# First slots and drain of a cross attention: other loads, lent buffers, unread products, new order

## The reference

```python
x = x + xattn(layernorm(x), ctx, lens, Wq, Wk, Wv, Wo, q_norm_w, k_norm_w)
x = x + attn(layernorm(x), w_qkv, b_qkv, w_out, b_out)
x = x + ffn(layernorm(x), w_gate, w_up, w_down)

def xattn(q, kv, lens, ...):        # q (4, 128, 512), kv (4, 2048, 512), 16 heads of 64
    qh, kh, vh = heads(q @ Wq), heads(kv @ Wk), heads(kv @ Wv)
    qh, kh = rms_norm(qh, q_norm_w), rms_norm(kh, k_norm_w)
    scores = einsum('bhld,bhsd->bhls', qh, kh) / sqrt(64)
    scores = where(arange(2048) < lens[:, None], scores, -1e9)
    return merge(softmax(scores) @ vh) @ Wo
```

## Time and profile before

| | |
|---|---|
| median of 3 runs | 1163.91 us (1163.73 to 1163.95) |
| the profiled execution | 1166.78 us, its span 1165.0 us |
| TensorE busy | 1135.1 us, 97% |
| VectorE busy | 837.2 us, 72% |
| POOL busy | 857.9 us, 74% |
| ScalarE busy | 739.9 us, 64% |

### The profile page before, as it was taken

The page is one execution under the profiler, slowest core; times in us unless marked ns, Lnnn a source line. Parts: engine busy times, 40 slices in busy tenths (PEclk is TensorE's granted clock), DMA queues, the critical chain, the costliest instruction groups (busy, mean ns, idle before and its releaser), DMA issues. The chain is left out here.

```text
span 1165.0 us, 29367 instructions
## 1 busy us (share of the span) xinstructions
PE 1135.1 (97%) x10783; PEld 868.0 (75%) x10783; DVE 837.2 (72%) x1953; ACT 739.9 (64%) x1335; POOL 857.9 (74%) x744
## 2 busy tenths in 40 slices
PE   7999999999999999999999999999999899999988
PEld 5777778887888888788888887888887578654433
DVE  7788788797767678777677787767665654753686
ACT  6366656776776767666666777666666535823761
POOL 4599999888989888798889878988888633540600
PEclk9999999999999999999999999999999999999999
DMA  8679999999999999999999999999999924786000
GB/s 232 154 143 190 216 189 185 200 230 232 200 202 207 199 197 222 216 197 201 205 206 195 193 229 200 186 199 210 205 187 197 263 69 118 137 232 140 1 1 36
DMA packets 560573, 210.36 MB, mean 181 GB/s; under 512 B 506800, under 2 KB 525232, under 8 KB 560432
## 3 DMA queue, kind: packets, MB, share of 16 engines
q1 hardware_dynamic: 538544, 168.64, 77.8%
q10 hardware_dynamic: 21888, 39.86, 12.7%
HBM read 66.79 MB, written 23.07 MB: 77 GB/s over the span
## 5 line engine op out<-in xcount | busy, mean ns | idle before, releaser
L155 PE MATMUL pair<-arena 128*128 128x256 f16 x2048 | 560.6, 274 | 9.4 <-DVE arena L703 8.7
L156 PE MATMUL pair<-arena 128*128 128x256 f16 x2048 | 559.5, 273 | 0.0
L157 PE MATMUL pair<-arena 128*128 128x256 f16 x2048 | 559.5, 273 | 0.0
L545 POOL TENSOR_TENSOR p_parts<-probs,p_parts 128x512 f16<-128x512 f32 x256 | 314.4, 1233 | 22.7 <-ACT p_parts L652 22.0
L749 DVE CUSTOM_DVE_ANT_0 probs<-bank,mask 128x512 f32<-128x512 f32 x256 | 175.3, 685 | 157.9 <-PE bank L917 145.2
L555 POOL TENSOR_TENSOR k_rinv<-k_ms,half_neg 128x8 f32<-128x8 f32 x128 | 211.8, 1655 | 80.7 <-DVE k_ms L764 80.3
L155 PEld LDWEIGHTS pair<-arena 128*128 128x128 f16 x2048 | 200.2, 98 | 83.7 <-issue 49.2
L157 PEld LDWEIGHTS pair<-arena 128*128 128x128 f16 x2048 | 200.7, 98 | 23.8
L156 PEld LDWEIGHTS pair<-arena 128*128 128x128 f16 x2048 | 200.6, 98 | 21.1
L656 ACT ACTIVATE k_lh<-k_n 128x512 f16<-128x512 f32 x128 | 80.5, 629 | 187.9 <-DVE k_n L772 186.2
L629 ACT ACTIVATE probs<-probs,neg_max 128x512 f32<-128x512 f32 x256 | 182.9, 714 | 10.7 <-DVE neg_max L758 10.7
(11 more groups left out here) (314 smaller groups left out, 1714.6 us busy)
## 6 DMA issues: line engine op xcount, KB each, us to landing
raws<-in_ctx_t_dram SPq DMA_DIRECT2D x58, 256.0 KB, 3.7
side_kept<-side_parts ACTq DMA_DIRECT2D x40, 256.0 KB, 5.3
arena<-side_kept SPq DMA_DIRECT2D x40, 256.0 KB, 4.6
w_kept<-ffn_turned ACTq DMA_DIRECT2D x36, 256.0 KB, 3.8
side_raw<-in_w_qkv_dram ACTq DMA_DIRECT2D x24, 256.0 KB, 3.4
arena<-w_kept SPq DMA_DIRECT2D x24, 256.0 KB, 5.0
pt<-p_parts SPq DMA_TRANSPOSE x240, 4.2
ffn_raw<-in_w_gate_dram ACTq DMA_DIRECT2D x12, 256.0 KB, 3.2
```

What stands on the lines that cost most here:

```text
L155: nc.tensor.matmul(to, x_hi[k], w_hi[k], start=(k == 0), stop=False)
L156: nc.tensor.matmul(to, x_hi[k], w_lo[k], start=False, stop=False)
L157: mm = nc.tensor.matmul(to, x_lo[k], w_hi[k], start=False, stop=(k == n - 1))
L545: nc.gpsimd.tensor_tensor(p_parts[n % PTS][:, 1, :], probs[n % PROBS][:, :], p_parts[n % PTS][:, 0, :], ALU.subtract).then_inc(p_lo_done, 1)
```

## The change

- The first 22 tiles fit without waiting: 8 halves of the buffers `p_parts` and `pt` are lent besides the 10 of `probs` and 4 of `raws`. 16 are loaded at once, six more behind the transposes of x; x of batch 0 is loaded behind the sixth tile instead of the third.
- In the list the query weights move behind the tenth context tile (slots 2 and 3), and the second group's weights one slot ahead. The first query unit is projected in slot 4 instead of 2, with its square and sum in the same slot; pairs 0 and 1 are scored in slots 9 and 10 instead of 8 and 9.
- Steps of x are put on other places between the tiles, and the steps of keys 0 to 2 on VectorE and ScalarE too. Sum and scale of each query unit stand ahead of the tiles of their slot.
- TensorE runs 36 products of a zeroed buffer nobody reads, then waits for the third high part and runs 4 more.
- Drain: in slots from 257 TensorE does out projection, turns, values, then scores (before: scores, turns, values, out projection); pairs 125, 126, 127 are scored in slots 257, 258, 260. POOL splits keys 127 ahead of a part. Residual of a batch comes a slot before its statistics; batches 0 and 1 one slot earlier; transposes by one slot closer. The weights of self attention are loaded three per slot from slot 258. A loop of warming products whose range of slots (257 to before 257) is empty is removed.

```diff
 CTX_RAWS, KTS, VS, PROBS, PTS, QS = 4, 3, 10, 10, 4, 3
...
 MASKS_AT = SCORE_LAG
+FIRST_SCORES = (SCORE_LAG + 2, SCORE_LAG + 3)
+WARM_FIRST, WARM_SECOND, EARLY_KEYS = 36, 4, 3
 FREE_AT = 120
-X0_AT = (2, 4, 5)
-Q_AT = {2: (0, 0), 18: (1, 0), 22: (2, 0), 26: (3, 0), 31: (0, 1), 35: (1, 1), 39: (2, 1), 43: (3, 1)}
+X0_AT = ((-1, 5), (0, 0), (1, 0))
+Q_AT = {4: (0, 0), 18: (1, 0), 22: (2, 0), 26: (3, 0), 31: (0, 1), 35: (1, 1), 39: (2, 1), 43: (3, 1)}
 Q_UNITS = list(Q_AT.values())
-OUT_FIRST, NORM_AT, WO_FIRST = (257, 261, 265), (261, 265), 249
+OUT_FIRST, NORM_AT, WO_FIRST = (257, 261, 265), (260, 264), 249
...
+        warm = mask[:, CHUNKS - 1, 0:P].bitcast(F16)
...
             ITEMS[t // 2 - 2] = [("c", 0, t), ("c", 0, t + 1)]
+        ITEMS[2] += [("q", 0, 0), ("q", 0, 1)]
+        ITEMS[3] = [("q", 0, 2), ("q", 0, 3)] + ITEMS[3]
         for j in range(4):
-            ITEMS[j // 2].insert(j % 2, ("q", 0, j))
             ITEMS[27 + j] = [("q", 1, j)]
-        ITEMS[6] = [("w", 0, 1), ("w", 1, 1)]
+        ITEMS[5] += [("w", 0, 1), ("w", 1, 1)]
         for group in range(2, GROUPS):
...
-            return probs[j][:, :].rearrange("p (k s) -> p k s", k=KD) if j < PROBS else ctx_raw[(j - PROBS) % CTX_RAWS]
+            if j >= FIRST:
+                return ctx_raw[(j - FIRST) % CTX_RAWS]
+            if j < PROBS:
+                return probs[j][:, :].rearrange("p (k s) -> p k s", k=KD)
+            i, of_pt = divmod(j - PROBS, 2)
+            lent = pt[i][:, :, :].rearrange("p a q -> p (a q)") if of_pt else p_parts[i][:, :, :].rearrange("p a k -> p (a k)")
+            return lent.bitcast(F32).rearrange("p (k s) -> p k s", k=KD)
 
...
-            return Q_UNITS.index(Q_AT[slot - lag]) if slot - lag in Q_AT else None
+            first = min(Q_AT)
+            if slot == first + (0, 0, 0, 1, 2, 3, 4, 5)[lag]:
...
         def pair_of_scores(slot):
 
-            if slot == SCORE_LAG + 1:
-                return 0
+            if slot in FIRST_SCORES:
+                return FIRST_SCORES.index(slot)
+            if slot > PARTS:
+                return LAST_SCORES.get(slot)
             d, odd = divmod(slot - SCORE_LAG, 2)
-            return d if 0 < d < PROJS and not odd else None
...
 
-            if slot == SCORE_LAG + 2:
-                return [0, 1]
+            if slot - 1 in FIRST_SCORES:
+                d = FIRST_SCORES.index(slot - 1)
+                return [2 * d, 2 * d + 1]
+            if slot - 1 in LAST_SCORES:
+                return [2 * LAST_SCORES[slot - 1], 2 * LAST_SCORES[slot - 1] + 1]
             n = slot - SCORE_LAG - 1
-            return [n] if 2 <= n < PARTS else []
+            return [n] if 2 * len(FIRST_SCORES) <= n < 2 * min(LAST_SCORES.values()) else []
 
...
             def load(j):
-                if j >= PROBS + CTX_RAWS:
...
 
-            for j in range(PROBS + CTX_RAWS):
+            for j in range(AT_ONCE):
...
+                    if n == 0:
+                        sp.wait_ge(item_lo_done, FIRST)
...
                 for item in split(slot):
-                    if PROBS + CTX_RAWS <= no[item] + CTX_RAWS < len(item_list):
+                    if FIRST + CTX_RAWS <= no[item] + CTX_RAWS < len(item_list):
...
                         sp.dma_start_transpose(xt0[i][:, :, b * P:(b + 1) * P], x_parts[:, i, :]).then_inc(xt0_in[b], 16)
+                    if b == 0:
+                        for j in range(AT_ONCE, FIRST + CTX_RAWS):
...
-                if (b := batch_at(5, slot)) is not None:
+                if (b := batch_at(4, slot)) is not None:
...
-                for j in range(GROUPS + 2 * (slot - PARTS), GROUPS + 2 * (slot - PARTS) + 2):
+                for j in range(GROUPS + 3 * (slot - PARTS - 2), GROUPS + 3 * (slot - PARTS - 1)):
...
+            nc.gpsimd.memset(warm, 0.0).then_inc(warm_ready, 1)
...
+                d = slot // 2 - 1
+                if slot > PARTS and slot % 2 == 0 and d - 1 < PROJS:
+                    keys_low(d - 1)
...
+                if slot <= PARTS and slot % 2 == 0 and 0 <= d - 1:
+                    keys_low(d - 1)
...
-                for i, item in enumerate(split(slot)):
-                    item_high(item)
-                    if slot == -1 and i == X0_AT[2]:
-                        x_high(0)
...
                 if (m := q_unit(1, slot)) is not None:
                     act.wait_ge(qp_done, m + 1)
...
+                if slot % 2 == 1 and 0 <= d < EARLY_KEYS:
+                    keys_high(d)
+                for i, item in enumerate(split(slot)):
+                    item_high(item)
+                    if (slot, i) == X0_AT[2]:
+                        x_high(0)
...
+                    if n == 0:
+                        act.wait_ge(item_lo_done, FIRST)
...
+                if slot % 2 == 1 and EARLY_KEYS <= d < PROJS:
+                    keys_high(d)
...
+                    wait(dve, q_ms_done, m - 1)
+                    nc.vector.tensor_reduce(q_ss[m % 2][:, :], q_sq, AX_X, ALU.add).then_inc(q_ss_done, 1)
...
                 for i, item in enumerate(split(slot)):
+                    if slot % 2 == 0 and 0 <= d < EARLY_KEYS - 1 and i == len(split(slot)) // 2:
+                        keys_normed(d)
                     item_low(item)
-                    if slot == -1 and i == X0_AT[0]:
+                    if (slot, i) == X0_AT[0]:
                         x_moments(0)
-                    if slot == -1 and i == X0_AT[1]:
...
                     dve.wait_ge(norm_in, 32)
                     nc.vector.scalar_tensor_tensor(norm_w[:, :], qk_norm[:, 0, :], Q_UP, qk_norm[:, 1, :], ALU.mult,
                                                    ALU.mult).then_inc(norm_done, 1)
...
                                                    ALU.mult, ALU.add).then_inc(r_done, 1)
...
+            def out_projected(slot):
+                for b in range(len(OUT_FIRST)):
+                    first = (slot - OUT_FIRST[b]) * 2
+                    if not 0 <= first < GROUPS:
+                        continue
...
+                    if first % 4 == 0:
+                        pe.wait_ge(side_in[first // 4], 64)
+                    for k in range(first, first + 2):
+                        hi, lo = (ot[:, b, i, k, :] for i in range(2))
...
+            def unread(times):
+                for i in range(times):
+                    nc.tensor.matmul(pair[0][:, 0, :], warm[:, 0:P], warm, start=True, stop=True)
+
+            pe.wait_ge(warm_ready, 1)
+            unread(WARM_FIRST)
+            pe.wait_ge(item_hi_done, 3)
+            unread(WARM_SECOND)
             for slot in range(LAST):
...
-                if PARTS + 1 <= slot < OUT_FIRST[0]:
-                    pe.wait_ge(k_n_done, PROJS - 1)
-                    pe.wait_ge(v_lo_done, PROJS - 1)
-                    for i in range(WARM_DRAIN):
-                        nc.tensor.matmul(bank[0][:, 0:4 * VW], ident16[:, :], v_both[0][:, 0, :, :, :].rearrange("p h a v -> p (h a v)"),
-                                         start=True, stop=True)
+                if slot <= PARTS:
+                    scored(slot)
+                out_projected(slot)
...
                 if slot > PARTS:
                     values(slot)
...
+                    scored(slot)
```

More of the change, by code:

```diff
@@ L877, in values, with scored @@
                     mm.then_inc(pv_done, 1)
+            def scored(slot):
+                if (m := pair_of_scores(slot)) is not None:
+                    u = m // CHUNKS
+                    pe.wait_ge(kt_in[m % 2], 16 * (m // 2 + 1))
+                    if u == 0:
+                        pe.wait_ge(q_turned_in, 16)
+                    elif m % CHUNKS == 0:
+                        pe.wait_ge(q_in[u % QS], 16 * ((u - (u % QS == 0)) // QS + 1))
+                    wait(pe, s_max_done, 2 * m)
+                    for i, (q_part, k_part) in enumerate(((0, 0), (1, 0), (0, 1))):
+                        for h in range(2):
+                            rows = slice(HD * h, HD * (h + 1))
+                            q_now = q_turned[rows, q_part, 0, :] if u == 0 else q_st[u % QS][rows, q_part, :]
+                            mm = nc.tensor.matmul(scores[h][:, :], q_now,
+                                                  kt[m % KTS][rows, TILES * k_part:TILES * (k_part + 1), :].rearrange(
+                                                      "p t k -> p (t k)"), start=(i == 0), stop=(i == 2))
+                    mm.then_inc(s_done, 1)
```

118 lines of the change are left out of this document (52 added, 66 removed).

## The result

The changed kernel takes 1169.17 us (median of 18 runs, 1164.06 to 1174.52), the kernel before, measured beside it, 1163.33 us: ratio 1.0049, interval [1.0034, 1.0065] (95%). It is 5.8 us slower where 1157.2 was forecast. The profiled execution of after took 1169.12 us around a span of 1167.3, at its own median; the profiled one of before stood 3.4 us over its median, so the traces differ by 2.3 us only (1167.3 against 1165.0). The medians here count every execution, and the ratios leave out three that ran far slower (one of 4130 us, and two of the kernel before with 1188 and 2416 us). A ratio and the quotient of two medians differ by up to 0.13%, 1.5 us.

The account below looks back on a forecast made before the run. TensorE, busy 97% of the span, was taken as the bound. Gains of 2.1 us in the first slots and 4.6 in the drain, 6.7 together, subtracted from the median 1163.91 gave 1157.2 us; range 1154.3 to 1161.2.

Parts of the forecast that it names:

- (a): First slots: unread products raise TensorE's clock before real work at 8.66 us, removing the slow stretch; 2.76 us won.
- From slot 11 to 256 each engine has the same instructions in the same slots: Middle of the kernel: taken as unchanged, query units' order within a slot moving by under 1 us of VectorE.
- (b): First slots: TensorE's waits on pair 2's keys and turned queries go (0.6, 1.1 us); VectorE walk adds 0.9 and 1.6.
- two weight tiles to 30.9: First slots, VectorE's walk: tiles 13, 14, 15 and two weight tiles done by 30.9 us, ahead of keys 2.
- a wait for k_n of over 3 us: Sign in the trace after, first slots: TensorE waiting this long for normalized keys would mean (A).
- (A): Rival: only the drain pays, VectorE's chain or a late tile 10 eats the front; 4.6 us, 1159.3; chance 0.22.
- Tile 10: First slots: in place at 21 to 22 us, split by 23.2, needed at 24.35; no wait, slack 1 us.
- The drain: After slot 256: waits of 2.25, 1.22, 0.66 and a slow clock removed, 5.6 us; 4.6 left, bounds 1.5 and 5.6.
- The 1.5 us for the clock: Drain: the slow stretch 904.76 to 908.42 takes 3.66 us and would take 2.15 at full clock.
- (D): Rival, slower: the drain's out projection waits for weights over about 6 us and holds back TensorE's queue; chance 0.03.
- -1 (keys 2 or the queries 3 us later than this): First slots: lower bound of their gain, forecast at 2.1 us with upper bound 4.4.
- Slower: Outcome class: the changed kernel measures slower than before; chance 0.03, against 0.07 for same and 0.90 for faster.

Follow-up runs that it names:

- drain alone: The kernel before with only the change's new drain and its old first slots: 1160.43 us, ratio 0.9968; run again later, 1159.12 us, 0.9976.
- experiments 3 to 6: Unread products varied: changed kernel without them 1161.61 us, 40 of 8 columns 1167.94, 40 late ones 1164.76, 127 short ones 1160.20; similar variants on the drain alone.
- experiment 2: Changed kernel with two more lent buffers, 1165.33 us (1.0014); changed kernel with two weight tiles split in slot 6 instead of 5, 1164.17 us (1.0016).
- front alone: The changed kernel with the drain of before, so only the new first slots: 1167.71 us, ratio 1.0039 to the kernel before.
- experiment 1: Changed kernel with the drain of before, 1167.71 us (1.0039); kernel before with the new drain, 1160.43 us (0.9968).

## Why the prediction was wrong

**(a) The slow stretch.** The mechanism was right, and its term too: 40 products of zeros raised the clock, with the change at 5.5 to 5.7 us and not at some 6.8 as by the forecast (1.09 + 5.70), and real work ran at the higher level from 8.17. In three other traces with the same 40 full products the change lies between 6.6 and 7.0 us. Wrong was that the step added nothing but this. "They have 7.6 us of otherwise idle time in front of them" counted only TensorE's time. The instructions themselves moved every later code load, and with them came a cost of 3 us on the drain alone and 4.5 to 7.7 on the changed kernel (experiments 3 to 6). The sentence "From slot 11 to 256 each engine has the same instructions in the same slots" is the step that failed with it: true of the slots, not of when their code comes and what it meets.

**(b) The walk through VectorE.** It put the waits at 0.9 and 1.6 us and keys 2, finished, at 34.7; measured were 0.19, 5.32 and 38.57 (37.88 + 0.69). Three things were missing. First, the "two weight tiles to 30.9" were taken as landed. They may load only when tiles 18 and 19 are split, went out at 27.07 and 28.27, and by the very rows I used for tile 10 (2.7 to 7.2 us) would land at 31 or later; 5.3 us came. Second, they stand ahead of the square of keys 2 on ScalarE, and I walked VectorE alone. Third, "the early halves of keys 0 to 2" were put among what costs nothing: they place passes of POOL beside VectorE's tiles, which then take 1.55 instead of 0.68 us (experiment 2). The wait then let the clock fall: from 38.63 to 43.22 us 4.6 us at 0.21 for work that takes some 2.4 at 0.11, a further 2.2. Slot 8 starts 3.1 us later than in before (38.63 against 35.57), the slow stretch adds 2.2, and the old wait of 1.0 for the turned queries is gone: 4.3, where pair 2 came 4.1 later. I had read from the earlier trace rows that a wait of 2.25 us lowered the clock and did not ask what a longer wait would do here. By the prediction's own sign a wait for k_n of over 3 us meant (A), 1159.3; the wait came, and the time did not. Even so the front without unread products comes out near even: changed kernel without them 1161.61, drain alone 1160.43, so it costs about 1.2 us (1.5 to 2.4 by the ratios, with intervals that overlap).

**Tile 10 and the first loads** were in time, as forecast. TensorE's wait of 0.66 us at 22.14 was for the tiles of the query weights, which I had not priced. The prediction took from the Trainium skill (DMA: Bandwidth & Descriptors, "Issuing engines are not separate DMA queues"), by which DMAs interleave on the same 16 engines, that two more loads at once could make the first tile up to 1.4 us later. That did not come: the first real product came at 8.17, before 8.66.

**The drain.** Right in its mechanism: the wait of 2.25 became 0.15, the stretch behind it runs at 1.00, 1.22 and 0.66 are gone, and in the trace of after there is no wait for `side_kept`. The size: forecast 4.6, 3.65 in the traces, 3.2 and 3.3 in the medians of the two runs alone. The 1.5 us for the clock was luck of the one trace: in the front alone the same wait left the clock up, and the old drain took 2.2 us less. Half a microsecond was set aside for the tail; the new waits there were 1.02 (POOL's low half of the last part) and 0.44.

**The sum.** 5.8 slower, by medians: drain -3.2, first slots without the unread products +1.2, the unread products +7.6; in sum 5.6. These are steps of one chain of kernels, so that they add up is no test, and their sizes hold for this order alone: in the front alone all first slots with the unread products cost 4.1, not 8.8. The slower rival (D) was in the drain and did not occur. No rival had the first slots as a loss, though the bound "-1 (keys 2 or the queries 3 us later than this)" named the place: keys 2 came 3.9 later. It had no price for the clock behind it. "Slower" had 0.03 since every case was summed over the two ends of a middle taken as fixed.

**Open.** Shown is that 40 added products cost and 127 do not, in two kernels, as the place of the code loads foretold, and that the packets then stand where they stood. No run moves the loads and nothing else, so that they are the cause is the reading that fits, not a proof. How a packet of 16 KB makes a later transpose 2.3 us longer is not shown: the long transpose of the 40 does not itself lie beside a code load. It may be the order in which transfers of other queues then fall. Nor is it shown how the 5 to 8 us split over the later places: in single traces the losses at 127, 276 and 497 us add up to 4.7, and those at 276 and 497 come and go between kernels. Why the two halves of the change don't add up (experiment 1) is open as well. And whether the clock falls behind a wait differed between traces that waited equally long, for 2.25 us in the drain and for 3.36 us in slot 8.

## What to carry to other kernels

Instructions added in idle time of one engine still move its whole instruction stream. Where transfers are tight, try other numbers of them (none, some, about one interval of the code loads) before the effect is put down to what the instructions do. Walk an edit through every engine that its chain crosses and every buffer that a load waits for, not through the bound engine alone, and price a wait with the clock that follows it. A gain at one end of a kernel is only a gain if the middle is shown to stand still, so read the start of the same work at several places. Measure both halves of a change alone and together: only the sum shows whether their effects are independent. And do not price a fall of the clock as certain from one trace.

## What the runs showed of the hardware

- Packets of 16 KB come on a queue of their own (q8, "instruction"), 86 or 87 in the span, 13 us and 124 products of TensorE apart in the mean. Added products move them; 40 cost 3 to 8 us of 1163 here, 127 nothing that is told apart.
- A VectorE pass with two tiles in SBUF beside a POOL pass of 128x512 took 1.55 us (after, 19.84) instead of 0.68, and POOL's 1.48 and 1.60 (19.36, 29.62) instead of 1.16 (before, 24.15).
- TensorE's clock, lower and higher level: in after up between 5.5 and 5.7 us where work began at 1.09; a wait of 5.32 us to 38.63, and 0.50 granted from 36.3 to 43.1; behind waits of 3.36 us 1.00 in one trace, 0.50 in another; behind the drain's wait of 2.25 us 0.66 over 904 to 909 in before and 1.00 in the front alone; behind a wait of 1.94 us 0.50 from 497.1 to 500.5 in after.
- 123 products of 8 columns took 3.44 us from 1.09 us on, 0.028 each, and did not raise the clock for the real work, which began at 7.88 with 0.17 and then 0.21 us between starts (drain alone with 127 short ones).
